# A four-layer graph network on one core: the source ranking moves from layer 0's gather pass to layer 1's scatter pass

## The chip, the cores and the metric

One NeuronCore of a Trainium2 chip runs the whole program. The time is device microseconds of one launch; the runs of this kernel are given with their median.

## The reference

6250 nodes with 64 features, 200,000 edges (`src`, `dst`), sorted by `dst`, with three edge attribute arrays. Four layers follow each other, each with a normalisation and a residual. Only the first two matter here:

```
# layer 0
aggr = segment_sum(x[src] * edge_weight[:, None], dst)         # then layer norm and residual
# layer 1: attention with a softmax over the edges that share a source
h = x @ W_lin; x_j = h[dst] + edge_attr5 @ W_edge
alpha = leaky_relu(h[src].att_i + x_j.att_j)
out = segment_sum(x_j * softmax_by_src(alpha), src)
```

Layer 0 sums by destination, so the given order of the edges serves it. Layer 1 sums by source, so each edge needs its position in source order. The kernel computes these positions itself, with a counting sort.

## The kernel before, in words

The 200,704 padded edges lie as 128 partitions of L = 1568. A chunk is T1 = 28 columns of all partitions, so a pass has 56 chunks, taken as 28 turns of two (buffers b = 0 and 1). The chip's GpSimd (POOL) moves rows by index, one indirect DMA for each column, 28 in a chunk, 1568 in a pass.

**The counting sort** has two parts. A *histogram step* takes SB = 7 columns: VectorE makes two one-hot tensors (`one_hots`, L251 and L253), TensorE adds their products (L307) and signals `hist_used`. 224 steps cover a key; two keys (`dst`, then `src`) make 448. A *ranking step* takes 7 columns too, and 224 of them cover the source key. VectorE picks the previous step's positions (L423, L425), makes running bases (L414, L416) and the one-hots of three steps ahead; TensorE transposes and compares (L351, L358, L363), counts (L348) and ranks (L375, L376); ScalarE copies between (L385, L386, L392). Each waits on the others in every step. A turn has TURN = 8 steps.

**Layer 0** is one block with two phases. In the first, each chunk has 16 histogram steps, then VectorE weighs the 28 gathered rows (`weigh_early`, L862) and scans them into running sums (`sum_rows`, L871); POOL's gathers (L822) go in pairs, each pair held by `hist_paced`, a wait on `hist_used`. That covers chunks 0 to 27 and all 448 steps. In the second phase each chunk has 8 ranking steps; ScalarE weighs the rows (L957), into `l0_data` in SBUF, and the scan reads that instead of the PSUM tile `l0_data_ps`. POOL's pairs are held by `Ranking.paced`. At the end the positions are written to DRAM (`pos_d`). `partition_nodes` (L710) runs once, between chunks. SP's queue loads indices, and clears and copies DRAM arrays; ScalarE's queue stores the sums. `collect_sums` (from L637) follows.

**Layer 1** first makes a node table (L1157 to L1173 on VectorE) while POOL scatters it (L1190). Then comes the scatter pass: for each chunk SP loads the spread rows and attributes and, in `targets`, the positions; ScalarE makes `keep` (L1255); VectorE copies the rows into the PSUM tile `l1_data` (L1280, L1281), makes the edge part of the score (L1282, L1285), scans (L1288), and adds the score (L1292); ScalarE fills the outgoing rows (L1259, L1260); POOL scatters 28 columns (L1303). Halfway through a chunk's scatters POOL waits for the other buffer's scatters to have landed and sets `free`, which the fill and the score of the next chunk wait for. TensorE does nothing in this pass. `source_order_sums` follows.

Of the kernel before, what the change touches and what calls it, by code (L numbers as in the profile page):

```python
# [11 lines left out]
I32 = mybir.dt.int32  # L12
BF16 = mybir.dt.bfloat16
ALU = mybir.AluOpType
# [3 lines left out]
P = 128  # L18
# [72 lines left out]
def build(nc, a, out):  # L91
# [41 lines left out]
    with top:  # L133
# [24 lines left out]
        node_w, edge_w, node_const = keep_tile("l1_node_w", [P, 2, H, F1 + 1]), keep_tile("l1_edge_w", [P, H, D5]), keep_tile("l1_const", [P, H])  # L158
        norm = Normalise(sem, "l01")
        ordering(nc, a, sem, dict(locals()))  # L160
        layer0(nc, a, sem, dict(locals()))
        layer1(nc, a, sem, dict(locals()))
# [96 lines left out]
PACE = 2  # L259


class Ranking:

    def __init__(self, s, sem, name, g, hists, iota_hist):

        self.hists, self.zero_b, self.iota_hist = hists, g["zero_b"], iota_hist  # L270
        self.iota_b, self.ident_b, self.not_upper_b = g["iota_b"], g["ident_b"], g["not_upper_b"]
        self.low, self.high = s.sb(f"{name}_low", [P, L + 3 * SB], BF16), s.sb(f"{name}_high", [P, L + 3 * SB], BF16)
        self.key = s.sb(f"{name}_key", [P, L], I32)
# [3 lines left out]
        self.low_tf = s.sb(f"{name}_low_tf", [P, HOT, SB * P])  # L277
        self.earlier = s.sb(f"{name}_earlier", [P, 2, SB, P], BF16)
        self.goes_on = s.sb(f"{name}_goes_on", [P, NT, SB + 1])
        self.before = s.sb(f"{name}_before", [P, 2, NT, SB + 1])  # L280
        self.picked = s.sb(f"{name}_picked", [P, SB, NT])
        self.pos_f = s.sb(f"{name}_pos_f", [P, L + SB])
        self.pos_i = self.part = s.sb(f"{name}_pos_i", [P, L], I32)
# [6 lines left out]
        self.hist_used, self.copied_f = sem(f"{name}_hist_used"), sem(f"{name}_copied_f")  # L290
        self.turned_ready, self.copied, self.same_ready, self.masked, self.counted, self.based, self.ranked, self.read, self.ready = (
            sem(f"{name}_{n}") for n in ("turned_ready", "copied", "same_ready", "masked", "counted", "based", "ranked", "read", "ready"))

    def hist(self, n):

        return self.rank[:, n].rearrange("p j c -> p (j c)")

    def hist_tensor_start(self, nc, pe, n):
        wait(pe, self.hot[0], L // SB // HOT * n + 1)
        nc.tensor.matmul(self.hist(n)[:, 0:NT], self.zero_b[:], self.zero_b[:, 0:NT], start=True, stop=False, skip_group_check=True)  # L300

    def hist_tensor(self, nc, pe, n, h):

        for r in range(TURN):
            wait(pe, self.hot[r % HOT], h * (TURN // HOT) + (L // SB // HOT * n + r // HOT + 1))
            for j in range(SB):
                last = nc.tensor.matmul(self.hist(n)[:, 0:NT], self.hot_low[:, r % HOT, j], self.hot_high[:, r % HOT, j],  # L307
                                        start=False, stop=False, skip_group_check=True)
            last.then_inc(self.hist_used, 1)

    def hist_vector_start(self, v, n):
        if n == 0:
            v.sem_inc(self.hist_used, HOT)
            v.memset(self.low[:, L:], 0.0)
            v.memset(self.high[:, L:], 0.0)
            v.drain()
        split_keys(v, self.key, self.part, self.low, self.high)

    def hist_vector(self, v, n, h):
        for r in range(TURN):  # L320

            wait(v, self.hist_used, h * TURN + (L // SB * n + r + 1))
            one_hots(v, self.hot_low[:, r % HOT], self.hot_high[:, r % HOT], self.iota_hist, self.low, self.high, self.at(h, r)).then_inc(self.hot[r % HOT], 1)
# [2470 lines left out]
```

## Time and profile before

| | us |
|---|---|
| median of 3 runs (11494.93 to 11647.08) | 11548.99 |
| the profiled execution's own span, first to last instruction | 11537.7 |
| busy: PE / VectorE / ScalarE / POOL | 3146.5 / 6821.8 / 4714.2 / 6567.8 |
| granted TensorE clock, mean of the span | 0.627 |

The shares of busy time are means over stages with different limits. The stages that the diff touches lie in the first 5040 us.

### The profile page before, as it was taken

The page shows a single profiled execution, that of the slowest core. Times are in us where ns is not written, and L with a number is a line of the kernel's source. Part 1 is how long each engine was busy: PE and PEld are TensorE (multiplying, and loading weights), DVE is VectorE, ACT ScalarE, POOL GpSimd, SP SyncE. Part 2 cuts the span into 40 slices and gives each one's busy share as a digit, 9 for nine tenths or more (in the row PEclk, how much of TensorE's full clock was granted, in tenths as well). Part 3 has the DMA queues.
Part 4 walks back from the last instruction along what each step waited for, and adds up shares of the span by engine and source line. Part 5 has one row for each costly group of instructions (what it writes and reads, how often), then busy time and mean ns, then how long its engine had stood idle before and what let it go on. Part 6 is the DMA issues. An engine that isn't in the chain of part 4 may idle for free. (4 is left out here: it accounts for less than half of the span.)

```text
span 11537.7 us, 92744 instructions
## 1 busy us (share of the span) xinstructions
PE 3146.5 (27%) x19432; PEld 2586.9 (22%) x19432; DVE 6821.8 (59%) x9436; ACT 4714.2 (41%) x6523; POOL 6567.8 (57%) x6626
## 2 busy tenths in 40 slices
PE   1111588882000000000023555555554200000002
PEld 1111477772000000000013444444443100000001
DVE  6777666664222311159962777777775566666664
ACT  1111466661211111137731666666662343334342
POOL 5656666665677777730023666666662466666663
PEclk9999767675555555555555677776775655555555
DMA  3332322222333323235522444444441666666662
GB/s 91 88 83 78 80 60 71 71 82 26 121 112 111 107 94 106 103 125 207 205 104 52 117 118 124 117 116 122 118 117 39 194 202 201 199 202 205 203 201 70
DMA packets 722783, 1395.92 MB, mean 121 GB/s; under 512 B 409552, under 2 KB 439453, under 8 KB 715095
## 3 DMA queue, kind: packets, MB, share of 16 engines
q0 software_dynamic: 287072, 587.19, 19.4%
q1 hardware_dynamic: 406786, 639.32, 17.0%
q10 hardware_dynamic: 28852, 168.65, 4.0%
q8 instruction: 21, 0.34, 0.0%
q14 instruction: 52, 0.42, 0.0%
HBM read 827.48 MB, written 602.51 MB: 124 GB/s over the span
## 5 line engine op out<-in xcount | busy, mean ns | idle before, releaser
L822 POOL DMA_INDIRECT l_rows<-in_x,l_idx x1568 | 1613.7, 1029 | 1010.1 <-issue 431.0
L2445 POOL DMA_INDIRECT l_rows<-table,l_idx x1568 | 1487.5, 949 | 1032.2 <-issue 483.2
L1925 POOL DMA_INDIRECT l_rows<-h,l_idx x1568 | 1540.3, 982 | 882.1 <-issue 442.4
L1303 POOL DMA_INDIRECT rows<-l_rows,l_idx x1568 | 1548.9, 988 | 554.0 <-issue 526.3
L1960 PE MATMUL l_made<-l_kv_w,l_rows_t 128*128 128x256 f32 x3136 | 1117.3, 514 | 1041.1 <-ACT l_kv L1990 402.5
L1960 PEld LDWEIGHTS l_made<-l_kv_w,l_rows_t 128*128 128x128 f32 x3136 | 761.2, 259 | 1279.5 <-issue 1147.1
L2521 ACT ACTIVATE l_lifted<-l_rows,l_up 128x256 f32<-128x256 f32 x1568 | 653.2, 463 | 824.0 <-DVE l_half_low L2473 527.1
L1698 PE MATMUL l_wide<-l_diag,l_ones 128*128 128x384 f32 x4 | 3.3, 926 | 3218.0 <-DVEq L1728 3218.0
L1259 ACT COPY l_rows<-l_run 128x1792 f32<-128x1792 f32 x56 | 191.6, 3421 | 1636.1 <-POOLq L88 1359.5
L1292 DVE TENSOR_TENSOR l_rows<-l_run,l_weights_ps 128x56 f32<-128x56 f32 x56 | 12.0, 215 | 1371.0 <-POOLq L88 1168.7
L1698 PEld LDWEIGHTS l_wide<-l_diag,l_ones 128*128 128x128 f32 x4 | 1.0, 312 | 3218.9 <-DVEq L1728 3218.9
L2087 DVE TENSOR_TENSOR_SCAN l_hold<-l_keep,l_hold 128x960 f32<-128x960 f32 x224 | 484.3, 2162 | 312.0 <-ACT l_hold L2004 153.9
L251 DVE TENSOR_TENSOR r_hot_low<-l_iota_ps,r_low 128x896 bf16<-128x896 f32 x448 | 485.2, 1083 | 293.3 <-remote 251.8
L376 PE MATMUL r_rank<-r_before,r_low_tf 128*128 128x49 f32 x3136 | 651.0, 355 | 27.3 <-issue 26.5
L1990 ACT COPY l_kv<-l_made 128x512 f32<-128x512 f32 x784 | 447.4, 596 | 500.0 <-PE l_made L1960 216.7
L1015 PE MATMUL l_root_psa<-identity,x 128*64 128x128 f32 x49 | 13.2, 421 | 2326.7 <-DMA l_root<-in_root 2326.7
L376 PEld LDWEIGHTS r_rank<-r_before,r_low_tf 128*128 128x128 f32 x3136 | 623.6, 259 | 29.2 <-issue 28.9
L923 ACT COPY l_out<-l_run 128x1792 f32<-128x1792 f32 x56 | 183.2, 3272 | 1020.3 <-DVE l_run L871 844.8
L1692 POOL DMA_INDIRECT l_total<-sums,end_idx_src x49 | 58.1, 1187 | 911.1 <-SPq L1687 896.5
L2479 DVE SCALAR_TENSOR_TENSOR l_quarter<-l_half_high,l_up,l_half_low 128x128 f32<-128x128 f32 x1568 | 444.4, 352 | 168.1 <-issue 132.3
L1015 PEld LDWEIGHTS l_root_psa<-identity,x 128*64 128x64 f32 x49 | 9.0, 202 | 2328.4 <-DMA l_root<-in_root 2327.5
L2108 DVE TENSOR_TENSOR_SCAN l_run<-l_scale,l_data 128x975 f32<-128x975 f32 x224 | 488.3, 2180 | 16.1
(393 smaller groups left out, 12672.9 us busy)
## 6 DMA issues: line engine op xcount, KB each, us to landing
sums<-l1s_out ACTq DMA_DIRECT2D x56, 1988.0 KB, 7.1
sums<-l_out SPq DMA_DIRECT2D x112, 924.0 KB
spread<-zeros SPq DMA_DIRECT2D x28, 3612.0 KB
l_spread<-spread SPq DMA_DIRECT2D x112, 903.0 KB
l1s_rows<-rows SPq DMA_DIRECT2D x56, 1008.0 KB, 4.7
spread<-zeros SPq DMA_DIRECT2D x56, 938.0 KB
l_spread<-spread SPq DMA_DIRECT2D x56, 938.0 KB
sums<-l_out ACTq DMA_DIRECT2D x56, 896.0 KB
```

What stands on the lines that cost most here:

```text
L251: v.tensor_tensor(hot_low, iota_b[:].unsqueeze(1).to_broadcast([P, SB, P]), low[:, at].unsqueeze(2).to_broadcast([P, SB, P]), ALU.is_equal)
L376: last = nc.tensor.matmul(self.rank[:, b, j, 0:NT], self.low_tf[:, r % HOT, j * P:(j + 1) * P], self.before[:, b, :, j], start=False, stop ...
L822: pool.indirect_dma_start(rows[:, b, t], None, a["x"], bass.IndirectOffsetOnAxis(ap=idx[:, b, t:t + 1], axis=0)) \
L1303: pool.indirect_dma_start(g["rows1_d"], bass.IndirectOffsetOnAxis(ap=idx[:, b, t:t + 1], axis=0), rows[:, b, t], None).then_inc(sent[b], 16)
L1925: pool.indirect_dma_start(rows[:, c.r, t, 0:C], None, g["h2_d"], bass.IndirectOffsetOnAxis(ap=idx[:, c.r, t:t + 1], axis=0)).then_inc(got[ ...
L1960: last = nc.tensor.matmul(made[:, n, j * 256:(j + 1) * 256], rows_t[:, q % 2, at:at + P], kv_w[:], start=True, stop=True)
L1990: nc.scalar.copy(kv[:, c.r, 2 * j:2 * j + 2, :, 0:C], made[:, n].rearrange("p (j s c) -> p j s c", j=2, s=2 * H)).then_inc(made_read[n], 1)
L2087: v.tensor_tensor_scan(held_, keep[:, c.b].rearrange("p f t -> p (f t)"), held_, 0.0, ALU.mult, ALU.add)
L2108: v.tensor_tensor_scan(run[:, c.b, h].rearrange("p f t -> p (f t)"), scale[:, h].rearrange("p f t -> p (f t)"), data[:].rearrange("p f t - ...
L2445: pool.indirect_dma_start(rows[:, b, t], None, g["table3_d"], bass.IndirectOffsetOnAxis(ap=idx[:, b, t:t + 1], axis=0)) \
L2479: v.scalar_tensor_tensor(out=quarter[:, j], in0=half_high[:, j], scalar=up[:, b, k * GROUP + j, 1:2], in1=half_low[:, j], op0=ALU.mult, op ...
L2521: last = nc.scalar.mul(lifted[:, n, j], rows[:, b, k * GROUP + j, 4 * C:], up[:, b, k * GROUP + j, 0:1])
```

## The change

- Layer 0 keeps only the histograms. Each of its 56 chunks has 8 histogram steps, and VectorE weighs and scans every chunk, always by the PSUM tile. POOL's gathers go in lots of four (PACE = 4), each lot held by one histogram step: lot n of chunk c waits for `hist_used >= 8c + n + 1`, and the count begins at 4.
- The low and high digits of the source keys stay in SBUF (`src_low`, `src_high`) until layer 1. Ranking turn 0 stands at the end of layer 1's node table block. Turns 1 to 27 stand in the scatter pass, four steps to a chunk, between the parts of the chunk's own work. The last two chunks have none.
- The ranking's working buffers overlay buffers of layer 1's later part. Its PSUM tiles take the whole of PSUM, so `l1_data`, `l1_dot` and the edge weights are now in SBUF.
- The positions are no longer written to DRAM and loaded back: `score` casts 28 of them for each chunk (from `pos_f` to `idx`), and `targets` is gone. The scatters are not paced.
- The semaphores are cleared once more, between `ordering` and layer 0.

```diff
-PACE = 2
+PACE = 4
# layer 0, POOL: all 56 chunks
+for t in range(T):
+    if t % PACE == 0:
+        wait(pool, hist.used, (h * 2 + b) * TURN + (t // PACE + 1))
+    pool.indirect_dma_start(rows[:, b, t], None, a["x"], ...)
# layer 0, VectorE
+def both(n, h):
+    for b in range(2):
+        hist.vector(v, n, h * 2 + b)          # 8 steps
+        weigh(h + HALF * n, b)
+        sum_rows(h + HALF * n, b)
...
+                hist.vector_end(v, n)         # in the last chunk of each key
+                counts.first_positions(v, g, k, hist.sums[n], n + 1)
# layer 0: ScalarE's turn(), the ranking loops of all engines and the store of pos_d are removed
# layer 1, node table block: each of ScalarE, TensorE, VectorE
+    ranking.vector_start(v, g["first"]["src"])
+    for r in range(TURN):
+        ranking.vector_step(v, 0, r)
# layer 1, scatter pass
-data = s.ps("l1_data", [P, W, T + 1])
+data = s.sb("l1_data", [P, W, T + 1])
+dot = s.sb("l1_dot", [P, T, H])
+with pe.Fori(1, LAST + 1) as turn:
+    for r in range(TURN):
+        ranking.tensor_step(nc, pe, turn, r)
...
+        for b in range(2):                    # ScalarE
+            ranking.scalar_step(nc, act, h + 1, b * STEPS)
+            keeps(h, b)
+            ranking.scalar_step(nc, act, h + 1, b * STEPS + 1)
+            fill(h, b)
+            ranking.scalar_step(nc, act, h + 1, b * STEPS + 2)
+            ranking.scalar_step(nc, act, h + 1, b * STEPS + 3)
...
+            for b in range(2):                # VectorE
+                ranking.vector_step(v, h + 1, b * STEPS)
+                hold(h, b)                    # copies into data, edge score, scan
+                ranking.vector_step(v, h + 1, b * STEPS + 1)
+                score(h, b)                   # waits for free[b]; casts the 28 positions
+                ranking.vector_step(v, h + 1, b * STEPS + 2)
+                ranking.vector_step(v, h + 1, b * STEPS + 3)
```

## Rows read from the trace of the kernel before

**Rows 1.** The page's head and its part 1, busy time by engine.

```profile
span 11537.7 us, 92744 instructions
PE 3146.5 (27%) x19432; PEld 2586.9 (22%) x19432; DVE 6821.8 (59%) x9436; ACT 4714.2 (41%) x6523; POOL 6567.8 (57%) x6626
```

**Rows 2.** Windows: stretch, its length, busy time (instructions) by engine, granted clock, DMA.

```profile
40.00:1250.00 1210.00, 204.59 (x3146) 156.36 (x3146) 866.58 (x1075) 146.74 (x63) 752.84 (x795) 1.00 0.31 84
1250.00:2680.00 1430.00, 1165.64 (x9893) 1055.60 (x9893) 925.87 (x1415) 913.21 (x1542) 860.83 (x774) 0.69 0.25 68
...
2940.00:5040.00 2100.00, 0.00 (x0) 0.00 (x0) 449.39 (x366) 382.65 (x167) 1549.86 (x1569) 0.50 0.30 104
```

**Rows 3.** Layer 0's gathers by source line: ns min/median/max, first and last start.

```profile
L822 POOL DMA_INDIRECT l_rows<-in_x,l_idx x795: 942/947/1797, 40.1 to 1249.5; - x199
L822 POOL DMA_INDIRECT l_rows<-in_x,l_idx x774: 942/947/4619, 1249.5 to 2620.5; - x194
```

**Rows 4.** Waits in 40 to 1250: us in total, times, longest us.

```profile
DVE r_hot_low L251 <- remote: 251.8, 57, 8.3
...
POOL l_rows L822 <- remote: 127.8, 52, 4.2
```

**Rows 5.** Groups by line and form, VectorE, to 5040: busy us, mean ns | idle before.

```profile
L251 DVE TENSOR_TENSOR r_hot_low<-l_iota_ps,r_low 128x896 bf16<-128x896 f32 x448 | 485.2, 1083 | 293.3 <-remote 251.8 <-PE r_rank L307 26.6 <-issue 14.8
L1288 DVE TENSOR_TENSOR_SCAN l_run<-l_keep,l_data 128x1914 f32<-128x1914 f32 x56 | 231.9, 4141 | 189.6 <-ACT l_keep L1255 189.6
L253 DVE TENSOR_TENSOR r_hot_high<-l_iota_ps,r_high 128x343 bf16<-128x343 f32 x448 | 226.2, 505 | 0.0
...
L1280 DVE COPY l_data<-l_spread 128x1848 f32<-128x1848 f32 x56 | 116.6, 2082 | 14.6 <-DMA l_attr<-sorted_attr 7.9 <-issue 6.7
...
L871 DVE TENSOR_TENSOR_SCAN l_run<-l_keep,l_data_ps 128x1856 f32<-128x1856 f32 x28 | 112.6, 4021 | 2.0
L862 DVE TENSOR_TENSOR l_data_ps<-l_rows,l_iota_ps 128x1792 f32<-128x1792 f32 x28 | 56.8, 2029 | 41.1 <-DMA l_rows<-in_x,l_idx 39.9
...
L710 DVE TENSOR_SCALAR_CACHE_REDUCE l_scratch_row<-l_ends_row,l_edge 128x3136 bf16<-128x3136 f32 x8 | 27.8, 3479 | 0.8
...
L446 DVE CAST r_pos_i<-r_pos_f 128x1568 int32<-128x1568 f32 x1 | 1.0, 977 | 0.1
```

**Rows 6.** Timeline of layer 0's first phase: start, us, engine, line.

```profile
336.77 4.02 DVE L871 TENSOR_TENSOR_SCAN l_run<-l_keep,l_data_ps 128x1856 f32<-128x1856 f32 x1
337.14 0.95 POOL L822 DMA_INDIRECT l_rows<-in_x,l_idx  x1 [0.31 <-issue]
```

**Rows 7.** Timeline of layer 0's second phase.

```profile
1357.75 1.07 DVE L251 TENSOR_TENSOR r_hot_low<-iota_b,r_low 128x896 bf16<-128x896 bf16 x1
1357.83 1.81 POOL L822 DMA_INDIRECT l_rows<-in_x,l_idx  x1 [0.31 <-issue]
...
1372.51 4.03 DVE L871 TENSOR_TENSOR_SCAN l_run<-l_keep,l_data 128x1856 f32<-128x1856 f32 x1
1372.70 4.59 POOL L822 DMA_INDIRECT l_rows<-in_x,l_idx  x1 [0.30 <-issue]
```

**Rows 8.** Layer 1's scatters by source line, first and last start.

```profile
L1303 POOL DMA_INDIRECT rows<-l_rows,l_idx x1568: 956/962/2612, 2943.0 to 5017.2; - x196
```

**Rows 9.** Waits in 2930 to 5040, the scatter pass.

```profile
ACT l_rows L1259 <- POOLq L88: 1359.5, 45, 33.7
POOL rows L1303 <- issue: 526.3, 1567, 1.8
```

**Rows 10.** Waits in 1250 to 2680, the ranking phase.

```profile
DVE r_picked L423 <- PE r_rank L376: 243.4, 98, 9.9
```

**Rows 11.** Timeline where layer 0's block ends and in the node table block.

```profile
2680.20 0.25 DVE L637 TENSOR_SCALAR l_tiles<-tile_base,cross_key_dst 128x49 f32<-128x49 f32 x1 [5.81 <-PEq L767]
...
2814.47 3.25 DVE L1173 MEMSET l_run<- 128x3828 f32 x1 [0.75 <-issue]
```

**Rows 12.** The node table's scatters by source line.

```profile
L1190 POOL DMA_INDIRECT spread<-l_node_rows,start_idx_dst x49: 984/984/1070, 2850.0 to 2914.3; - x49
```

More of the change, by code:

```diff
@@ L289, in __init__, with spare @@
         self.hot = [sem(f"{name}_hot{r}") for r in range(HOT)]
[L290 to L323, printed above, removed]
-    def hist_vector_end(self, v, n):
-        v.wait_ge(self.hist_used, L // SB * (n + 1) + HOT)
+        self.copied_f = sem(f"{name}_copied_f")
+        self.turned_ready, self.copied, self.same_ready, self.masked, self.counted, self.based, self.ranked, self.read = (
+            sem(f"{name}_{n}") for n in ("turned_ready", "copied", "same_ready", "masked", "counted", "based", "ranked", "read"))
+    @classmethod
+    def spare(cls):
+        return cls.LOW_T + cls.BEFORE + cls.GOES_ON + cls.PICKED + cls.POS
     @staticmethod
@@ L616, in sort @@
                         ranking.vector_end(v)
+                        v.tensor_copy(pos_i[:], ranking.pos_f[:, SB:])
+                        v.drain().then_inc(ready, 1)
                     branch(v, g, sort)
@@ L803, in _, with gather @@
                     sp.wait_ge(x_in, 16)
[L804 to L806 removed]
                 @block.gpsimd
                 def _(pool):
[L810 to L814 removed]
+                    def gather(h, b):
                         wait(pool, idx_in[b], (h + 1) * 16)
@@ L1123, in layer1 @@
         edge_rows = s1.sb("l1_rows", [P, 2, T, R1])
+        scratch = [t[:].rearrange("p b h f t -> p (b h f t)") for t in (held.scale, held.run)]
+        ranking = Ranking(s1, sem, "l1r", g, g["src_low"], g["src_high"], scratch[1])
         with ExitStack() as stack:
@@ L1148, in _ @@
                     nc.scalar.copy(rows[:, :, 0:C], x[:]).then_inc(copied, 1)
+                    ranking.scalar_start(nc, act)
+                    for r in range(TURN):
+                        ranking.scalar_step(nc, act, 0, r)
+                @block.tensor
+                def _(pe):
+                    ranking.tensor_start(nc, pe)
+                    for r in range(TURN):
+                        ranking.tensor_step(nc, pe, 0, r)
                 @block.vector
@@ new lines, in fill @@
+                    def fill(h, b):
+                        wait(act, scanned[b], h + 2)
+                        wait(act, free[b], h + 1)
+                        nc.scalar.copy(rows[:, b, :, 0:C].rearrange("p t f -> p f t"), run[:, b, 0:C, 1:])
+                        nc.scalar.copy(rows[:, b, :, C:C + D5], attr[:, b]).then_inc(filled[b], 1)
+                    with act.Fori(0, LAST) as h:
+                        for b in range(2):
+                            ranking.scalar_step(nc, act, h + 1, b * STEPS)
[4 more added lines that the diff above has]
+                            ranking.scalar_step(nc, act, h + 1, b * STEPS + 3)
```

321 lines of the change are left out of this document (150 added, 171 removed).

## The prediction, made before the changed kernel ran

> **What bounds the kernel now.** The page's head gives 11537.7 us, of which POOL is busy 6567.8 and VectorE 6821.8, neither near the whole [rows 1]. So I read the stretches that the change touches one by one [rows 2]. Three of them matter: layer 0's first phase (1210 us), its second (1430 us), and layer 1's scatter pass (about 2080 us). In the first two POOL has 795 and 774 gathers, each 0.947 us by its median [rows 3] with a gap of 0.31 us to the next [rows 6], so 1.25 us apiece. 1568 of these are 1960 us; layer 0 takes 2640. So POOL isn't what fills layer 0. In the first phase VectorE is busy 867 of 1210 us, and 252 us of its idle time stand before the one-hots, released by "remote", a signal whose sender the trace doesn't resolve [rows 4, 5]; I read these as late signals on `hist_used`, on which POOL's pairs wait as well. In the second phase TensorE is busy 1166 of 1430 us at a granted clock of 0.69, and VectorE's longest waits are on its rank matmuls [rows 2, 10]: the chain of ranking steps sets the time, 1430 / 224 = 6.4 us a step, 51 us a chunk.
>
> Layer 1's scatter pass is another matter. Its scatters run from 2943.0 to 5017.2 [rows 8], 37.05 us a chunk, and POOL has no wait but the 0.3 us of issue and one of 1.8 us [rows 9]. ScalarE waits 1360 us for POOL there, and TensorE does nothing. POOL's issue rate is the bound.
>
> So the question is what moving the ranking leaves of layer 0, and what it adds to the POOL instructions of layer 1.
>
> **Layer 0: 56 chunks of 8 histogram steps.** VectorE's work in one chunk is 8 x (1.083 + 0.505) = 12.7 us of one-hots, 2.03 of weighing and 4.02 of scan [rows 5], with small copies about 19.5 us. POOL's is 28 x 1.25 = 35.0. POOL becomes the bound if the gates let it. Lot n of a chunk needs step n - 4 of that chunk, since the count starts at 4. Lots 0 to 3 need steps of the chunk before, long done. Lot 4 needs this chunk's first step, and VectorE gets there after it has weighed and scanned the chunk before: some 3 us of landing (an estimate without a row), 6 of work and 1.6 for the step, about 11 to 12 us after POOL's last gather of that chunk. By then POOL is in its tenth gather of sixteen. So no gate binds, by 8 us a chunk. What would take this cover away is a late signal; the longest in the trace is 8.3 us [rows 4].
>
> Three single costs. `partition_nodes` holds VectorE for 8 x 3.48 = 28 us between two chunks [rows 5]; step and lot 4 then come at 12 + 28 = 40 us, where POOL was there at 20, so 20 us. Splitting the source keys and `first_positions` are some 10 us of VectorE and fit into its 15 us of slack. The new clearing of semaphores before layer 0 is bound by 0 and by about 10 us, a quarter of the 40.1 us that pass before the first gather; I take 5.
>
> POOL's last gather then starts at 40.1 + 5 + 1960 + 20 = 2025 us. Behind it come landing, weighing and the scan (9 us), and from there to the collect about 9 as in the trace, where the collect starts at 2680.2 [rows 11] after the last scan of 4 us. So the collect starts at 2043, 637 us earlier. The late signals: POOL's "remote" waits are 127.8 us in 28 chunks [rows 4], 4.6 a chunk, while its gates were tight at every second gather. All of that in 56 chunks would be 256 us, the upper end; the lower is nothing. I take 20, nearer to nothing, because VectorE's steps now come in a burst early in the chunk, ahead of the gates that need them. **Layer 0: -617 us, between -637 and -380.**
>
> **The node table block.** Ranking turn 0 is 8 steps of up to 6.4 us behind VectorE's last memset, which ends at 2817.7 [rows 11]: 2870. POOL's table scatters run until 2914.3 [rows 12] and cover it. Without that cover it would cost some 50 us. I put 4 us for scatters that meet one-hots.
>
> **Layer 1's scatter pass.** The chunk's own chain grows by four ranking steps. With all in a row: 4 x 6.4 = 25.6, copy and scan 2.1 + 4.1 [rows 5], small operations 1.2, the wait on ScalarE's `keep` 189.6 / 55 = 3.4 [rows 5], the fill about 3.8 (an estimate, by its tile nearly that of `keep`): 40 us, and part of it overlaps, since a step on TensorE may run beside VectorE's hold. POOL gives it 37 us or more and half a chunk of notice by `free`. So the chain stays hidden, though without much room.
>
> What isn't hidden is POOL itself. Layer 0's trace has the experiment ready. In the first phase the scan reads one SBUF tile and one PSUM tile, and a gather that starts 0.37 us into it takes 0.95 us [rows 6]. In the second phase the scan's two inputs are both in SBUF, and a gather that starts 0.19 us into it takes 4.59 us, until the scan is over [rows 7]; the maxima of the two phases differ so (1.8 and 4.6 us) [rows 3]. A gather that starts 0.08 us into a one-hot with both inputs in SBUF takes 1.81 us instead of 0.95 [rows 7]. The change puts `l1_data` into SBUF, so every chunk has such a scan, of 4.14 us, and every ranking chunk four such pairs of one-hots, with no pacing.
>
> The Trainium skill, "SBUF — State Buffer", section "SBUF: two separate sides", has a rule for this: VectorE and GpSimd share one port pair by an exclusive lock, and a VectorE instruction with two SBUF inputs takes it from a GpSimd instruction that reads SBUF. It speaks against this change, and the trace agrees for gathers that start inside such an instruction; by the rule as it stands the lock holds both ways for a whole instruction, so the sum would be the same or a little higher.
>
> Scan: 4.59 - 0.95 = 3.64 us lost in each chunk, 56 times, 204 us. One-hots: the loss is nothing if no scatter starts inside one and 0.9 us if one starts at its beginning. With one start every 1.265 us and a window of about 0.94 us the mean over phases is 0.94 x 0.94 / 2 / 1.265 = 0.35; I take 0.3 per step, 4 x 0.3 x 54 = 65 us, between 0 and 194. The copy L1280 now writes SBUF: it keeps its 2.08 us [rows 5] or falls to about half, by the cast L446, whose 1568 elements from SBUF to SBUF take 0.98 us [rows 5]. Either may hold POOL: 0 to 80 us, I take 22. The skill's "VectorE: DVE Perf Modes", section "Mode 2×_2P — use both read ports for one tensor", says that such a copy reads with both ports; by it the copy is short and locks, which the 22 us allow for. POOL's one idle stretch of 1.8 us in a chunk [rows 9], the wait for the other buffer's landings, has more time to pass in a slower chunk; up to 84 us could come back, and I take none. `targets` and the store of the positions go, off POOL's path and SP's queue: nothing. **Layer 1: +291 us, between +120 and +480.**
>
> **Sum.** On the profiled execution 11537.7 - 617 + 4 + 291 = 11216. The median of the runs is 11 us above that execution, so 11227, rounded to 11230.
>
> **The rivals.**
> 1. *Late signals keep layer 0 gated.* POOL doesn't get its 35 us a chunk but some 40, as the phase of today spends 4.6 us of "remote" waits on each chunk, and all of it stays: -380 instead of -617, 11465. For it: nothing shows what delays the signals. Against: only lots 4 to 6 can be hit. 0.13.
> 2. *The scatters always meet the one-hots.* POOL's phase against VectorE is set anew at every `free` and every scan, so the phases may repeat in each chunk, badly: +480, 11420. 0.06.
> 3. *The ranking chain sets layer 1's pass: the slower end.* The chain of 40 us holds if signals are in time. If one of two ranking steps in a chunk gets a signal late by the 8.3 us of [rows 4], it is 40 + 17 = 57 us, 56 x 57 = 3190 us against 2074, +1116, and with layer 0's gain the whole is near 12050. It decides from 37 + 617 / 56 = 48 us a chunk on; below that the sum is a gain. For it: TensorE, idle there today at a clock of 0.50 [rows 2], will run its steps cold, and late signals are in the trace wherever it takes part. Against: in the ranking phase 8 steps and a scan took only 51 us, late signals and ScalarE's weighing included. 0.10.
> 4. *Nothing in layer 1 stretches.* The scatters read their index and rows from SBUF, but by another road than the gathers write: then only the -617 stay, 10930. For it: no scatter of today meets a scan with two SBUF inputs, so the trace can't show it. Against: a scatter and a gather are the same instruction with 0.96 and 0.95 us [rows 3, 8]. 0.05.
>
> **How the numbers follow.** The forecast has 0.66; its own range is 11080 to 11400. Together with the rivals, 11060 to 11520 leaves out rival 3 (0.10), rival 4 (0.05) and some 0.05 at the edges. A measurement of this kernel tells about 2% from no change, 231 us: faster is below 11318. Of the forecast's 0.66 some 0.57 lie there, with rival 4 that is 0.62. Same: the rest of the forecast and rivals 1 and 2, 0.28. Slower: rival 3, 0.10.
>
> **What the changed profile would show.** Layer 0's gathers 1.25 us apart almost without waits, the collect near 2045 to 2065, and VectorE idle before the weighing, for the gathers to land. In the scatter pass one scatter of about 4.6 us in each chunk, starting just inside the scan, a scatter maximum near 4.6 and a mean near 1.1; 42 to 43 us a chunk; ScalarE and VectorE still waiting for POOL, but less. If instead the fill waits for the scan and POOL for the fill, rival 3 is it. The prediction is wrong if the gates bind in layer 0, or if the chain of ranking steps outgrows POOL's chunk.

## The result, and the profile after

The changed kernel takes 12129.64 us (median of 4 runs, 12120.07 to 12151.12), the one before 11544.1 us beside it (4 runs). The ratio is 1.0526 [1.048, 1.0573]: slower, where 11230 was forecast. The profiled execution has a span of 12120.3 us against 11537.7 us, 582.6 us more.

The starts of two groups of DMAs cut both spans into comparable stretches. First the page of the kernel after, with the groups that answer to [rows 3, 5, 8]:

```profile
L1308 POOL DMA_INDIRECT rows<-l_rows,l_idx x1568 | 1599.9, 1020 | 1388.3 <-DVE l_idx L1281 873.8
```

and its two source lines, with first and last start:

```profile
L823 POOL DMA_INDIRECT l_rows<-in_x,l_idx x1568: 938/944/1797, 40.6 to 2313.2; - x196
L1308 POOL DMA_INDIRECT rows<-l_rows,l_idx x1568: 952/958/4761, 2635.3 to 5569.4; - x196
```

| stretch | before | after | difference |
|---|---|---|---|
| to layer 1's first scatter | 2943.0 | 2635.3 | -307.7 |
| first to last scatter | 2074.2 | 2934.1 | +859.9 |
| last scatter to the end | 6520.5 | 6550.9 | +30.4 |

The scatters take 52.4 us a chunk (before: 37.0), yet GpSimd is busy in them for only 51 us more than before (1599.9 against the 1548.9 that the page of before gives for L1303; a second trace of the kernel before, r6 below, has 1591.7). The pass isn't stretched by longer scatters but by GpSimd standing still: 56 pauses of over 2 us between its scatters come to 874 us, most of them 20.1 us long. Who stands before it shows in the waits of that stretch, 2640 to 5560 (us in total, times, longest):

```profile
DVE l1s_run L439 <- remote: 1501.2, 79, 40.6
ACT l1r_earlier L408 <- remote: 913.8, 86, 32.9
POOL rows L1308 <- DVE l_idx L1281: 820.5, 43, 25.1
ACT l1r_low_t L401 <- remote: 537.3, 55, 23.5
PEld l1r_same L379 <- issue: 523.3, 257, 17.1
```

In [rows 9] ScalarE waited 1360 us for GpSimd. Now GpSimd waits for VectorE, and VectorE for a signal whose sender the trace doesn't resolve ("remote"). I call such a wait one for a late signal. L439 waits only on `ranked`, L408 on `same_ready` (and on ScalarE's own `copied_f`) and L401 on `turned_ready`; those three are TensorE's. In the first 2340 us the same reading:

```profile
DVE r_hist_low L255 <- remote: 792.7, 93, 15.3
POOL l_rows L823 <- remote: 274.8, 76, 7.5
```

The timeline of the kernel after shows what TensorE does meanwhile (start, us, engine, line, operation, idle time before it). GpSimd issues one scatter every 1.26 us without a break until 3636.34; of its rows only the last one of the run stands here:

```profile
3608.91 0.96 PE L367 MATMUL l1r_turned<-ident_b,l1r_hot_low 128*128 128x128 bf16 x7
...
3612.57 0.23 PE L391 MATMUL l1r_rank<-l1r_hot_high,l1r_earlier 128*128 128x49 bf16 x1
...
3613.72 0.46 PE L392 MATMUL l1r_rank<-l1s_run 128*128 128x49 f32 x2 [0.92 <-issue]
3613.85 0.92 ACT L408 ACTIVATE l1r_earlier<-l1r_same 128x896 bf16<-128x896 f32 x1 [7.68 <-remote]
...
3615.86 0.43 PE L392 MATMUL l1r_rank<-l1s_run 128*128 128x49 f32 x1 [0.47 <-issue]
...
3625.78 0.91 ACT L401 COPY l1r_low_t<-l1r_turned 128x896 bf16<-128x896 bf16 x1 [11.02 <-remote]
...
3626.83 0.91 PE L379 MATMUL l1r_same<-l1r_low_t 128*128 128x128 bf16 x7 [8.37 <-ACT l1r_low_t L401]
...
3632.00 0.24 PE L364 MATMUL l1r_count<-l1r_hot_high,l1r_hot_low 128*128 128x49 bf16 x1 [1.86 <-issue]
...
3634.10 0.24 PE L364 MATMUL l1r_count<-l1r_hot_high,l1r_hot_low 128*128 128x49 bf16 x1 [1.86 <-issue]
...
3635.39 0.95 POOL L1308 DMA_INDIRECT rows<-l_rows,l_idx  x1 [0.30 <-issue]
...
3640.40 0.69 PE L367 MATMUL l1r_turned<-ident_b,l1r_hot_low 128*128 128x128 bf16 x5 [0.43 <-issue]
3640.59 0.52 DVE L439 TENSOR_TENSOR l1s_run<-l1r_rank,l1r_hot_high 128x343 f32<-128x343 f32 x1 [28.64 <-remote]
3640.74 0.92 ACT L408 ACTIVATE l1r_earlier<-l1r_same 128x896 bf16<-128x896 f32 x1 [9.86 <-remote]
```

The seven matmuls of L364 need nothing new once `hot` is there, and elsewhere they run as one group of x7 in 0.8 us. Here single ones come 2.1 us apart, each after 1.86 us in which TensorE waits for nothing that the profile knows. Some 4 us after the end of GpSimd's last scatter everything comes through at once.

The same rows show a second thing: signals come late for matmuls that the profile has already ended. The seven transposes of L367 end at 3609.87, and ScalarE's L401, which waits for their signal alone, starts at 3625.78. The last rank matmul (L392) of a step ends at 3616.29, and VectorE's L439 starts at 3640.59. The ends of matmuls are modelled, so the trace can't say whether the work or the signal was late. A signal to TensorE in the same run of scatters was in time: L401 ends at 3626.69, and L379 starts at 3626.83.

That is the rule, not an accident: VectorE has 46 "remote" waits of over 15 us in the pass, 1278 us together. 40 of them end while GpSimd stands still, 36 of these 3.3 to 5.2 us after its last scatter, and its next scatter is then typically 16 us away; 6 end inside a run of scatters. So a chunk mostly goes: 28 scatters in a row (35 us), 4 us until TensorE's signals arrive, 16 us until the next chunk's rows and targets are ready. The ranking's work no longer runs beside the scatters but largely behind them.

### The profile page after: what moved, and what is told of

It reads as the page before. It is cut to its first block and busy times, and to the rows that moved or that the text cites. A ratio compares the mean times of both kernels' runs of the same rounds, so it can differ in the third digit from the quotient of the medians.

```text
span 12120.3 us, 91009 instructions
## 1 busy us (share of the span) xinstructions
PE 3362.7 (28%) x19432; PEld 2705.6 (22%) x19432; DVE 6858.8 (57%) x9546; ACT 4526.9 (37%) x5718; POOL 6470.0 (53%) x6626
## 5 line engine op out<-in xcount | busy, mean ns | idle before, releaser
L1308 POOL DMA_INDIRECT rows<-l_rows,l_idx x1568 | 1599.9, 1020 | 1388.3 <-DVE l_idx L1281 873.8
L823 POOL DMA_INDIRECT l_rows<-in_x,l_idx x1568 | 1480.7, 944 | 832.1 <-issue 471.9
L439 DVE TENSOR_TENSOR l1s_run<-l1r_rank,l1r_hot_high 128x343 f32<-128x343 f32 x225 | 114.7, 510 | 1701.2 <-remote 1555.1
L255 DVE TENSOR_TENSOR r_hist_low<-l_iota_ps,src_low 128x896 bf16<-128x896 f32 x448 | 486.1, 1085 | 932.9 <-remote 792.7
L392 PE MATMUL l1r_rank<-l1s_run 128*128 128x49 f32 x3136 | 715.5, 359 | 373.9 <-issue 372.5
L392 PEld LDWEIGHTS l1r_rank<-l1s_run 128*128 128x128 f32 x3136 | 680.9, 273 | 379.7 <-issue 379.1
L287 PE MATMUL l_hist<-r_hist_high,r_hist_low 128*128 128x49 bf16 x3136 | 202.3, 216 | 2025.0 <-DVE r_hist_high L257 1157.6
L287 PEld LDWEIGHTS l_hist<-r_hist_high,r_hist_low 128*128 128x128 bf16 x3136 | 154.5, 115 | 2072.8 <-issue 2072.8
L408 ACT ACTIVATE l1r_earlier<-l1r_same 128x896 bf16<-128x896 f32 x224 | 205.4, 917 | 1034.9 <-remote 966.7
```

Of the source, the lines that this page charges most:

```text
L255: v.tensor_tensor(hot_low, iota_b[:].unsqueeze(1).to_broadcast([P, SB, P]), low[:, at].unsqueeze(2).to_broadcast([P, SB, P]), ALU.is_equal)
L392: last = nc.tensor.matmul(self.rank[:, b, j, 0:NT], self.low_tf[:, r % HOT, j * P:(j + 1) * P], self.before[:, b, :, j], start=False, stop ...
L823: pool.indirect_dma_start(rows[:, b, t], None, a["x"], bass.IndirectOffsetOnAxis(ap=idx[:, b, t:t + 1], axis=0)) \
L1308: pool.indirect_dma_start(g["rows1_d"], bass.IndirectOffsetOnAxis(ap=idx[:, b, t:t + 1], axis=0), rows[:, b, t], None).then_inc(sent[b], 16)
```

## The experiments

The comparisons fell into two groups. In one, the kernel before took 11544 to 11673 us, as in the times given. In the other it took 10380 to 10386 us; between the two lie 11%, within the first group 1%. I call them 11,600 sessions and 10,380 sessions. Chip number seven appears in both, so what sets them apart isn't its number. The traces show one difference: the nine of 10,380 sessions have no "remote" wait at all, in the whole execution, while the eleven of 11,600 sessions have 1542 us (before) to 4950 us (the changed kernel) of them, all engines together. Each run is compared with the kernel before of its own session. r1 to r4 had expectations for an 11,600 session only, so their totals in us can't be met; from r5 on most have one for either kind. Theory A is that GpSimd's runs of indirect DMAs delay TensorE; theory B that the chain of ranking is too long by itself; theory C that port conflicts on SBUF do it. ("Rival C" in the expectations of r11 and r13 is another: that traffic on the DMA engines does it.) A pause is idle time of over 0.6 us between two of GpSimd's DMAs, and a run is what lies between two pauses.

**First session, of the 10,380 kind (before 10383.8).**

`r1_sbuf_only`, the kernel before with the one part of the change that moves tiles out of PSUM:

```
-            data = s.ps("l1_data", [P, W, T + 1])
+            data = s.sb("l1_data", [P, W, T + 1])
...
+            dot_sb = s.sb("l1_dot", [P, T, H])
+            edge_w_ps, dot = g["edge_w"][:], dot_sb[:]
```

> The kernel before, with l1_data, l1_dot and the edge weights of layer 1 in SBUF and nothing else changed. It prices the port conflict alone. My term in the prediction: one scatter of each chunk is held for the length of the scan, 3.6 us x 56 = 204 us, and up to 1.4 us more a chunk by the copy: about 11750 to 11830, scatter maximum 4.6 us or more. If conflicts on SBUF inputs are not what lengthens layer 1 (POOL is busy only 51 us longer there after the change), the time is within 60 us of the kernel before.

`r2_rank_first`, the change with all ranking steps ahead of the scatter pass (VectorE's part; ScalarE's and TensorE's are changed alike, and the steps in the pass are gone):

```
-                    for r in range(TURN):
-                        ranking.vector_step(v, 0, r)
+                    with v.Fori(0, NC // 2) as h:
+                        for r in range(TURN):
+                            ranking.vector_step(v, h, r)
```

> The changed kernel, with all 224 ranking steps in the node table block, ahead of the scatter pass, so that POOL issues no DMA beside most of them. Theory A (a long run of indirect DMAs from POOL delays TensorE's signals, and that stretches the ranking chain): the steps go at 4 to 6.4 us, 900 to 1400 us in all, with hardly any wait named remote, and the scatter pass falls back to 37 to 42 us a chunk. Theory B (the chain of the ranking is itself too long, whatever POOL does): steps of 8 us or more, 1800 us, waits named remote as today. The total is between 12000 and 12500 by A, over 12800 by B.

`r3_lots7`, the change with gates in layer 1's scatters:

```
                         for t in range(T):
+                            if gated and t and t % 7 == 0:
+                                wait(pool, ranking.ranked, ranking.at(h + 1, b * STEPS + t // 7) + 2)
...
```

> The changed kernel, with layer 1's scatters held in lots of seven, lots 1 to 3 each by a ranking step of the chunk (POOL waits for the signal of its rank matmuls). Theory A: runs of scatters are broken, the late signals shrink from 7 to 30 us to a few, a chunk takes 42 to 47 us instead of 52.4, total 11550 to 11850. Theory B or theory C (the port conflict): more waits for POOL and nothing gained, 12130 or more.

`r4_lots4`, the same with lots of four, held by `ranked` and `hot` in turn:

> As the lots of seven, but lots of four scatters, each held by a rank signal or by the one-hots of a step, as the ranking phase of the kernel before holds its gathers. Theory A: the shorter runs leave fewer late signals still, chunk 40 to 45 us, total 11450 to 11750, at or below the lots of seven. Theory B or C: 12130 or more.

Measured: r1 10621.53 us, ratio 1.0242 [1.0214, 1.027]; r2 11155.74 us, 1.0749 [1.0727, 1.0772]; r3 10453.58 us, 1.0069 [1.0043, 1.0095]; r4 10464.13 us, 1.0086 [1.0065, 1.0107]. The scatters by source line, r1 and then r3:

```profile
L1301 POOL DMA_INDIRECT rows<-l_rows,l_idx x1568: 954/958/4754, 2635.5 to 4888.5; - x196
```

```profile
L1310 POOL DMA_INDIRECT rows<-l_rows,l_idx x1568: 953/958/4779, 2333.7 to 4708.2; - x196
```

What follows. The first scatter of r1, whose layer 0 is that of before, starts at 2635.5, and that of r3 at 2333.7: the change gives 302 us in layer 0. GpSimd is busy 1756.8 us in r1's scatters, 208 more than in those of before and 165 more than in r6's; 55 of them take over 3 us, 181 us more than 0.96 each. The conflict of C is real: it costs one scatter a chunk up to 4.75 - 0.96 us, and r1 in all 237.7 us, inside its expected 200 to 280. r3's page has 1879.7, 331 more: the one-hots and the rest add 123. Its waits in 2333 to 4710 show that the gates hardly held GpSimd (0.3 us), and that VectorE's waits for TensorE were short and had a name:

```profile
POOL rows L1310 <- issue: 495.1, 1565, 1.8
DVE l1s_run L439 <- PE l1r_rank L392: 353.0, 79, 7.0
```

1879.7 + 495.1 is the whole pass of 2374.5, or 42.4 us a chunk. There is no late signal in it, so such a session can't show the loss of the result at all. r4's gates held as little. In r2 VectorE had its 216 steps in the 833 us during which GpSimd waited, 3.9 us a step; the ranking's cost was then added in full.

**Second session, of the 11,600 kind (before 11616.81).** `r5_after` and `r6_before` are the two kernels unaltered, `r7_lots7` is r3 again. `r8_ungated_l0` takes the gates out of layer 0:

```
-                            if t % PACE == 0:
-                                wait(pool, hist.used, (h * 2 + b) * TURN + (t // PACE + 1))
```

> The changed kernel, nothing altered, beside before on one chip. Theory A (TensorE's signals arrive late under long runs of GpSimd's indirect DMAs, by an amount that differs between chips): where before takes near 10,380 us, the ratio is 1.00 to 1.02 (10,400 to 10,560 us) and the scatters of layer 1 take 2300 to 2400 us, as with the gated lots (2374.5); where before takes near 11,545 us, the ratio is 1.045 to 1.06, the scatters take 2850 to 2950 us, and VectorE's scan of bases waits for TensorE's signals for over 1000 us in all. Theory B (the chain of ranking plus layer 1's own work is too long by itself, on any chip): the ratio is 1.04 or more on either, with the scatters at 2800 us or more, and most of GpSimd's wait is behind VectorE's and ScalarE's busy time, not behind signals.

> The kernel before, nothing altered, profiled on the chip of this call, so that its stages can be laid beside those of the changed kernel. Theory A: near 10,380 us layer 0's gathers end near 2635 less 300 = 2300 us and later waits for unnamed releasers are below 5 us at the longest; near 11,545 us they end near 2620, with the long waits of the first profile. Theory B makes no difference between chips beyond the clock: waits for TensorE's signals are the same share of the span.

> The changed kernel with layer 1's scatters issued in lots of seven, each held until the next ranking step has been counted. Theory A on a chip where before takes near 11,545 us: the gates break the long runs of scatters, late signals get rarer, and the scatters take 2450 to 2750 us, so 11,650 to 11,950 us in all, faster than the unaltered change by 150 to 500 us; on a chip where before takes near 10,380 us no gate matters: 10,430 to 10,480 us again, within 0.5% of the unaltered change. Theory B: no gain from the gates on either chip, for a gate can only add a wait: the same as the unaltered change or up to 100 us slower.

> The changed kernel with layer 0's gathers not held by histogram steps at all (the gates of four taken out). If the gates cost nothing, as the terms of the prediction have it, the time is within 20 us of the unaltered change and layer 0's 3584 gathers take the same. Rival (the gates protect VectorE's and TensorE's chain from a run of gathers): layer 0 gets 50 to 300 us longer where signals arrive late, and the same where they don't. Other rival (the gates hold GpSimd): layer 0 gets shorter by up to 46 us, what they were seen to wait.

Measured: r5 12132.84 us, 1.0527 [1.0425, 1.0629]; r6 11639.93 us in one run; r7 11741.81 us, 1.018 [1.0084, 1.0276]; r8 12389.16 us, 1.0762 [1.0645, 1.0879]. The scatters of r6, r7 and r8, one fence for each:

```profile
L1303 POOL DMA_INDIRECT rows<-l_rows,l_idx x1568: 955/962/2612, 2958.5 to 5080.6; - x196
```

```profile
L1310 POOL DMA_INDIRECT rows<-l_rows,l_idx x1568: 952/958/6370, 2627.4 to 5194.6; - x196
```

```profile
L1306 POOL DMA_INDIRECT rows<-l_rows,l_idx x1568: 954/962/5627, 2864.4 to 5845.3; - x196
```

The same gates that held nothing in the other kind of session save 391 us here: r7's pass takes 2567 us where r5's takes 2938 (2632.4 to 5570.3). They split the runs of 28 into mostly 7 and 21, with 113 pauses of 289 us together. A gate can only add a wait, so B, by which gates can't help, falls. r8 says the same of layer 0: without gates the first scatter starts 232 us later (2864.4 against 2632.4), although gathers then never wait for a gate. Holding GpSimd makes the kernel faster. r6 is the check on all this: its pass takes 2122.1 us against 2074.2 in the first trace of the same kernel, so differences of some 50 us between two traces mean nothing. C falls as the main cause too, for GpSimd's busy time is 1598.5 us in r5 and 1835.9 us in the faster r7.

**Third session, of the 10,380 kind (before 10380.41).** `r9_lots4_pairs0` is r4 with layer 0's gathers held in pairs:

```
-                            if t % PACE == 0:
+                            if t % 4 == 0:
                                 wait(pool, hist.used, ...)
+                            elif t % 2 == 0:
+                                wait(pool, hist.hot[(t // 4) % HOT], (h * 2 + b) * (TURN // HOT) + (t // 4 // HOT + 1))
```

> The changed kernel with both stages paced more closely: layer 1's scatters in lots of four, each held by a ranking step, and layer 0's gathers in pairs, by histogram steps and their one-hots. Theory A (TensorE's instructions come slowly while GpSimd issues a long run of indirect DMAs, and catch up in its pauses), where before takes near 11,600 us: layer 1's scatters take 2400 to 2570 us (lots of seven: 2567), layer 0's gathers end 0 to 100 us earlier than at 2627, and the time is 11,560 to 11,760 us. Where before takes near 10,380 us: 10,440 to 10,500 us, as with the lots of four before. Theory B (the chain is too long by itself): the lots cost as much as they give; layer 1's scatters take 2850 us or more where before takes near 11,600 us.

`r10_gaps` has no gate, but pauses:

```
                         for t in range(T):
+                            if t and t % 4 == 0:
+                                pool.memset(gap[:], 0.0)
+                                pool.drain()
```

> The changed kernel with no gate in layer 1, but with a filling of a small tile and a drain by GpSimd after every four scatters, so that each run of scatters has pauses whatever the ranking does; nothing waits for the filling. Theory A, where before takes near 11,600 us: pauses of 1 us are time in which TensorE's instructions come through, so VectorE's wait for late signals falls from 1598 us to below 1000 us and the scatters take 2450 to 2800 us in place of 2937. Theory B: the pauses (six a chunk, some 6 to 10 us) lie beside the chain or add to it, never shorten it: 2937 to 3300 us. Where before takes near 10,380 us both say 2374 us or up to 150 us more.

`r11_direct` leaves the sorting scatter out:

```
-                        for t in range(T):
-                            pool.indirect_dma_start(g["rows1_d"], ..., rows[:, b, t], None).then_inc(sent[b], 16)
+                        pool.dma_start(g["run_of"](g["rows1_d"], R1)[:, bass.ds((h * 2 + b) * (T * R1), T * R1)],
+                                       rows[:, b].rearrange("p t w -> p (t w)")).then_inc(sent[b], 16)
...
```

`free` is then set once the other buffer's DMA has landed.

> The changed kernel with layer 1's 28 indirect scatters of a chunk replaced by one ordinary DMA of the same tile, issued by GpSimd: rows of layer 1 are then stored in the order of the edges and not sorted by source node, so the output isn't the reference's; all other work of the stage stays, and the same bytes are written. Theory A: without runs of indirect DMAs the signals are in time on any chip, and the stage's 56 chunks take the chain's own 26 to 34 us each, 1450 to 1900 us. Rival C (the traffic on the DMA engines delays TensorE, not GpSimd's instructions): late signals stay over half of what they were, 2200 us or more where before takes near 11,600 us. Theory B: 2800 us or more, for the chain is whole.

`r12_tight` is r3 with `+ 3` in place of `+ 2`, a lot waiting for one ranking step more:

> As the lots of seven, but each lot waits for one ranking step more, so that GpSimd goes in step with the ranking and stops after each lot. Theory A, where before takes near 11,600 us: fewer late signals than with the looser gates, layer 1's scatters take 2400 to 2560 us (looser: 2567), in all 11,570 to 11,740 us; where before takes near 10,380 us, the chain of 42.4 us a chunk sets the pace and the gates add 0 to 100 us. Theory B: a tighter gate only adds waits: 2600 us or more on either.

Measured: r9 10891.75 us, 1.049 [1.0458, 1.0522]; r10 11138.81 us and r11 9542.65 us in one run each; r12 10463.23 us, 1.008 [1.0057, 1.0103]. Two misses, a good number and one that tells nothing:

- r9 is 428 us slower than r4. Its page names the pairs' own wait, 472.1 us for `hot`; the scatters of layer 1 are as in r4. The gate at the middle of each lot was tight where I had taken it for loose.
- r10's pass takes 3053 us, 679 more than r3's; I had allowed 150. The 336 fillings take 236.0 us, and the drains 523 us of idle time (1018.0 of issue against 495.1), while the scatters take 78 less. GpSimd sets this pass in this kind of session, so all of a pause counts.
- r11's 56 chunks go from 2335.3 to 3813.8, 26.9 us a chunk. The chain of copy, scan, fill and four ranking steps is far below GpSimd's 42.4 us.
- r12's gates never held GpSimd, as r3's: its pass takes 2374.6 us.

**Fourth session, of the 11,600 kind (before 11672.79):** r11's kernel and the changed one again.

> The changed kernel with layer 1's 28 indirect scatters of a chunk replaced by one ordinary DMA of the same bytes (rows stored in the order of the edges, so the output isn't the reference's), once more, for the chip that the last call gave was one on which no signal is late; there the chain alone took 26.9 us a chunk, 1478 us from the first to the last chunk. Theory A, on a chip where before takes near 11,600 us: without runs of indirect DMAs TensorE's signals come in time there too, and the stage takes 1480 to 1750 us. Rival C (the stage's traffic on the DMA engines delays TensorE): over half of the late signals stay, 2200 us or more. Where before takes near 10,380 us: 1478 us again, and nothing is told apart.

> The changed kernel, nothing altered. Where before takes near 10,380 us: Theory A says that GpSimd alone sets layer 1's pass there, as with the gated lots: the scatters take 2350 to 2400 us and the time is 10,420 to 10,470 us, ratio 1.004 to 1.009; a rival (the gates themselves had helped there too) says 10,550 us or more. Where before takes near 11,600 us: 12,120 to 12,190 us, ratio 1.043 to 1.06 again.

Measured: r13 10641.08 us in one run, r14 12158.61 us, 1.0426 [1.0391, 1.0461]. The DMAs of r13, and VectorE's wait in 2700 to 4400 in the same trace:

```profile
L1307 POOL DMA_DIRECT2D rows<-l_rows x56: 531/533/591, 2630.8 to 4106.4; - x56
```

```profile
DVE l1s_run L439 <- PE l1r_rank L392: 187.9, 84, 3.3
```

So the chain takes 26.8 us a chunk in an 11,600 session too, and in the whole stretch there is not one "remote" wait, whereas layer 0 of the same execution has 816.0 us of them at L255. The DMA engines move twice as much in 2640 to 4100 (145 GB/s, share 0.37) as in the unaltered pass (73 GB/s, 0.20 in the kernel after), so the bytes moved aren't what delays TensorE. The 1568 indirect scatters are, and r15 asks whether it is their number or their order. TensorE's clock isn't it either: the granted share in the pass is 0.56 after the change with its late signals, and 0.59 in r10, where not one is late.

**Fifth session, of the 11,600 kind (before 11641.37):** r10's, r12's and the changed kernel again.

> The changed kernel with a filling of a small tile and a drain by GpSimd after every four scatters of layer 1 (2.25 us a pause on the other kind of chip, where the scatters took 3053 us). Where before takes near 11,600 us: Theory A with the length of a run as what counts: the pauses let TensorE's instructions through, the waits for late signals fall below 500 us, and the pass is GpSimd's own 3050 to 3150 us, in all 12,150 to 12,350 us. Rival (each scatter delays TensorE, pauses or none): late signals stay near 1500 us and add to the pauses, 3300 us or more. Where before takes near 10,380 us: 3053 us again.

> The changed kernel with layer 1's scatters in lots of seven, each held until the ranking is one step further than with the looser gates. Where before takes near 11,600 us: Theory A with the length of a run as what counts: each lot is followed by a pause, the waits for late signals fall, and the scatters take 2400 to 2560 us (looser gates: 2567), in all 11,570 to 11,740 us. Rival (each scatter delays TensorE): no better than the looser gates, 2570 us or more. Where before takes near 10,380 us: 2375 us again.

> The changed kernel, nothing altered. Where before takes near 10,380 us: GpSimd alone sets layer 1's pass, as with the gated lots: the scatters take 2350 to 2400 us, the time is 10,420 to 10,470 us, ratio 1.004 to 1.009. Where before takes near 11,600 us: ratio 1.04 to 1.06 again.

Measured: r15 12232.52 us in one run; r16 11725.94 us, 1.0063 [1.0036, 1.009]; r17 12199.55 us, 1.0459 [1.039, 1.0528]. The scatters on the page of r15 (they start from 2631.4 to 5685.2), and what its waits have left of late signals in the pass:

```profile
L1312 POOL DMA_INDIRECT rows<-l_rows,l_idx x1568 | 1830.3, 1167 | 1093.6 <-issue 1038.2
```

```profile
ACT l1r_low_t L401 <- remote: 13.6, 13, 2.4
ACT l1r_earlier L408 <- remote: 6.6, 2, 3.3
```

r15 keeps every scatter and only breaks the runs: most are four long, the longest eight, with pauses of 2.2 us between them. 20.2 us of "remote" waits remain of r17's 3065, and the pass takes 3053.8 us where r10's took 3053 in the other kind of session. Without late signals the two kinds agree in this stretch to a microsecond. So it is the unbroken run that counts, not the number of scatters. Its 336 pauses cost as much as the late signals had: r15 is no faster than r17.

r16's time lies in my interval, but not for my reason. VectorE's "remote" waits in 2640 to 5200 are still 1063 us (r17: 1394), and the runs between pauses aren't shorter: the gates on `ranked` are mostly open when GpSimd comes to them, and the median run is 28 scatters long, as in r17. The pass still takes 2536.5 us against r17's 3015.7 (2934 to 2941 in the three other traces of the changed kernel). What has changed is the pause behind a run. In r17 it is 20.1 us, for GpSimd goes on until its filled rows run out and then waits for the signals and for all the work behind them. In r16 it is 3.7 us (median of 55, 224 us together; 41 of GpSimd's waits, 164.3 us, are for a late signal at a gate), for the gate stops GpSimd while the rest of a chunk's rows lie ready, and it goes on as soon as the signal is there.

**Sixth session, of the 10,380 kind (before 10385.66):** `r18_pauses`, a cheaper pause in both stages:

```
+                            if t in (0, 9, 19):
+                                pool.drain()
```

> The changed kernel with a drain on GpSimd (a pause of some 1.5 us) before the first, tenth and twentieth DMA of each chunk, in layer 0's gathers and in layer 1's scatters. Where before takes near 11,600 us: Theory A: runs of nine or ten are short enough that late signals mostly vanish; layer 1's scatters take GpSimd's own 2375 us and 56 times three pauses, 2600 to 2700 us in place of 2937; layer 0, whose chain has room for the pauses, ends up to 296 us earlier (2335 to 2500 in place of 2630); in all 11,450 to 11,750 us, ratio to before 0.98 to 1.01. Rival (only pauses after every four do it, or the pauses cost as much as they free): 11,900 us or more. Where before takes near 10,380 us: layer 0's gathers take 0 to 60 us more and layer 1's scatters 200 to 300 us more than 2375.

Measured: 11323.36 us, 1.0898 [1.0879, 1.0916]. Its page:

```profile
L1312 POOL DMA_INDIRECT rows<-l_rows,l_idx x1568 | 1882.8, 1201 | 961.2 <-issue 932.5
L825 POOL DMA_INDIRECT l_rows<-in_x,l_idx x1568 | 1482.3, 945 | 995.6 <-issue 931.1
```

Both expectations of r18 for this kind are missed. A drain costs 2.6 us ((932.5 - 495.1) / 168), not 1.5, and layer 0 had no room either: +434 us until the first scatter. r18 was not run in an 11,600 session, so what three pauses do there stays open. No version that computes the reference beat the kernel before in either kind; the nearest are r16 at 1.0063 and r3 at 1.0069.

## Why the prediction was wrong, point by point

- **Layer 0, forecast -617 us (bounds -637 and -380), measured -308.** The picture of unhindered gathers was right as far as it went. From 2943.0, less 617, plus 4, the first scatter was due at 2330; in the 10,380 session (r3) it starts at 2333.7, gathers wait 29.0 us for gates, 22.0 of them once behind `partition_nodes` (forecast 20), and the weighing waits 936.5 us for the gathers to land, as forecast. That the two agree within 4 us is partly luck: r3's last gather starts 19 us later than the 2025 of the sum, and from there to the first scatter it takes 289 us where the trace of before has 322. But late signals were put at 20 us with 256 as the end, and the kernel after has 274.8 us of them on GpSimd alone. "VectorE's steps come in a burst ahead of the gates" failed: the burst itself waits 792.7 us for `used`. The gates of four hardly break the gathers there: the median run is 23 gathers long, against 9 and 4 in the two phases of before. Rival 1 was meant for this; it left a gain of 380, 72 us more than there was. In the 10,380 session the gain is 302, for the layer 0 of before is itself 300 us shorter there.
- **Table block and turn 0 (+4): fine.** From the last gather to the first scatter it takes 322.1 us after the change and 322.5 before. The clearing of semaphores (+5) shows nowhere: the first gather starts at 40.6, before at 40.1.
- **GpSimd's conflict in layer 1: right in kind and size where signals are in time.** In r1 and r3 the scan holds one scatter in nearly each chunk (55), to 4.78 us at the most (forecast 4.59), with 165 to 208 us in r1 against 204. All of it was +291 in the forecast, 42.2 us a chunk; r3 shows 42.4, GpSimd 331 us busier and its pass 300 us longer than that of before. In the changed kernel itself, whose VectorE stands waiting while GpSimd's runs go on, only 13 scatters take over 3 us. The Trainium skill, "SBUF — State Buffer", section "SBUF: two separate sides", has VectorE and GpSimd exclude each other on a shared port pair; the runs agree for scatters, with the 55 long ones of r1. The copy (L1266) now takes 1.86 us, not half of 2.08, so of the two ends I had given it the first was near.
- **"The chain stays hidden": the step that failed.** I summed 40 us for it out of rows that held late signals; without them it is 26.9 us (r11, r13). So its length was not the error; the overlap was. With runs of scatters beside it the chain gets its signals only in the pauses, a chunk becomes 28 scatters and 20 us behind them, and that is 52.4 us. The prediction treated a late signal as an accident of 8.3 us at the longest, "in the trace", but it had read that from the first phase alone: in 1250 to 2680 VectorE has one of 13.3 us and ScalarE one of 13.1. r7, r13 and r15 show that in 11,600 sessions late signals come from GpSimd's runs. Beside the ranking of before they were mostly four or eight gathers long; the change lets 28 scatters go in a row, and the longest wait rose to 40.6 us.
- **Rival 3 is what happened.** It gave 57 us a chunk and about 12050, with 48 as its turning point; measured 52.4 and 12130. Its mechanism, "a signal late by 8.3 us in one of two steps", had the right place and sign, and a price from the wrong rows. That its 12050 came within 80 us of the time is luck: it priced the pass 256 us too high and took 309 us too much for layer 0's gain. It got 0.10 because the ranking phase of before "took only 51 us, late signals included", but that phase was paced in pairs, and the gates that went away had kept its runs, and so its late signals, short.
- **The sum of what was seen.** -308 in layer 0, +860 in the pass, +30 behind it: +582, as the spans have it. The 860 can be split by r3's pass, in which no signal is late: 300 for GpSimd's own longer pass (2374.5 - 2074.2) and 560 for late signals (2934.1 - 2374.5). The split is an estimate, for r3 is of the other kind of session, in which the pass of before wasn't traced. Without the 560 the sum would be +22, and r3 measured +70 (1.0069), the same within 2%. So the forecast gain of some 300 us would not have come even without late signals in the pass.
- **Open.** What sets the two kinds of session apart; by which road a run of indirect DMAs reaches TensorE (the trace shows only that its instructions and its signals come late); and the unaltered change in a 10,380 session, which was never met. r3's gates hardly held GpSimd there, so it should be near 1.007, but that is argued, not shown.

## What to carry to other kernels

A gate that seems to cost an engine time may be what keeps another engine fed: before loosening the pacing of GpSimd's indirect DMAs, look for waits "released by remote" and for single matmuls spaced by idle "issue" time, and test whether they go away when the runs are broken, as in r15 (runs of four to eight: 20 us of them). If a run must be long, stop it while its next rows lie ready: r16 has runs as long as r17's and a pass 479 us shorter. Price a chain of small steps with its signals as late as unbroken runs make them, not as late as they are under the pacing that the change removes. And find out whether the cost appears in every session: here the same gates were worth 391 us in one kind, and in the other they hardly held anything (0.3 us).

## What the runs showed of the hardware that wasn't expected

- In an 11,600 session TensorE's instructions came as far as 2 us apart while GpSimd issued indirect DMAs without a pause, beginning some ten scatters into a run (3601 to 3636 us in the kernel after), and recovered about 4 us after the run. In the 10,380 sessions no signal of TensorE's came late, with up to 113 scatters in a row (r3).
- In the same rows TensorE's signals reached ScalarE and VectorE 16 and 24 us after the end that the profile gives their matmuls, while one from ScalarE reached TensorE in 0.14 us.
- One ordinary DMA of 1008 KB a chunk from GpSimd (0.53 us of its time) had no such effect, at twice the traffic.
- A drain on GpSimd between indirect DMAs cost 2.6 us.
- A scatter that starts inside VectorE's scan with both inputs in SBUF takes up to 4.78 us (r3), as gathers did in [rows 7].
